# Taking over the last attention output and the first expert loads across a stage border, and moving one batch's sum and moments into layer 1

## The reference, cut to what matters

```python
x = L0_attn_X                                   # (4, 1024, 128)
xn = layernorm(x)
s = attention(xn, W_qkv, W_out)                 # 16 heads of 64
g = silu(moe(xn, router, 8 experts, top 2, shared expert))   # squared-ReLU MLPs, d_ff 512
x = x + s * g
xn = layernorm(x)
s = ssm(rmsnorm(xn) * norm_w, dt, A, Bmat, C, D)  # 64 states, causal decay filter
g = silu(ffn_fp4(xn, w_gate, w_up, w_down))     # FP4 block quantising, inner size 352
x = x + s * g
```

## Time and profile before

| | us |
|---|---|
| median of 3 runs | 1923.96 (1921.51 to 1924.07) |
| profiled execution, time | 1938.15 |
| its span | 1936.3 |
| PE busy | 1811.3 (94%) |
| DVE busy | 1512.7 (78%) |
| POOL busy | 1432.3 (74%) |
| ACT busy | 1002.9 (52%) |
| granted TensorE clock, mean | 0.98 |

### The profile page before, as it was taken

How to read it: one execution, slowest core, us unless ns; L and a number is a source line. 1 busy time by engine, 2 the same in 40 slices (tenths; PEclk the granted TensorE clock), 3 DMA queues, 4 the chain that set the end, 5 groups by cost and what they waited for, 6 DMA issues and landing times. The chain is left out here.

```text
span 1936.3 us, 33414 instructions
## 1 busy us (share of the span) xinstructions
PE 1811.3 (94%) x10522; PEld 1039.0 (54%) x10522; DVE 1512.7 (78%) x2052; ACT 1002.9 (52%) x1503; POOL 1432.3 (74%) x870
## 2 busy tenths in 40 slices
PE   5899999999999999999999999999999798985687
PEld 4455555555555555555555555555555476763456
DVE  6777777777777777777777777777777688879896
ACT  4345545445454454554544454545445488874553
POOL 4388888888888888888888888888888256655574
PEclk9899999999999999999999999999999899997899
DMA  7101010101001010101010110101010467531000
GB/s 245 45 12 55 12 57 16 54 22 43 31 35 54 11 54 11 54 12 58 15 54 22 43 35 32 54 11 54 11 54 12 164 217 223 171 93 57 1 17 28
DMA packets 98438, 108.95 MB, mean 56 GB/s; under 512 B 8161, under 2 KB 88097, under 8 KB 95202
## 3 DMA queue, kind: packets, MB, share of 16 engines
q1 hardware_dynamic: 93410, 98.26, 15.6%
q0 software_dynamic: 4992, 10.27, 1.5%
HBM read 53.12 MB, written 27.38 MB: 42 GB/s over the span
## 5 line engine op out<-in xcount | busy, mean ns | idle before, releaser
L1438 POOL TENSOR_TENSOR psum_k<-psum_k,probs 128x1024 f32<-128x1024 f32 x384 | 925.9, 2411 | 200.4 <-ACT probs L1383 185.3
L1455 DVE TENSOR_REDUCE mxh<-ps_m 128x2 f32<-128x1024 f32 x518 | 633.3, 1223 | 257.0 <-PE ps_m L1215 255.8
L1383 ACT ACTIVATE probs<-ps_s 128x1024 f32<-128x1024 f32 x512 | 497.2, 1023 | 265.7 <-PE ps_s L1232 212.9
L1240 PE MATMUL ps_v<-probs,V 128*64 128x512 f32 x2056 | 489.8, 597 | 0.0
L1479 DVE RECIPROCAL rden<-den 128x128 f32<-128x128 f32 x260 | 245.7, 946 | 25.2 <-ACT den L1352 16.0
L1240 PEld LDWEIGHTS ps_v<-probs,V 128*64 128x64 f32 x2056 | 137.5, 137 | 235.6 <-issue 229.7
L1215 PE MATMUL ps_m<-k_hi,q_hi 64*128 64x512 f32 x1036 | 237.6, 453 | 11.2 <-DVE mxh L1455 7.2
L1230 PE MATMUL ps_s<-q_lo,k_hi 64*128 64x512 f32 x1024 | 202.7, 390 | 0.0
L1230 PE MATMUL ps_s<-q_hi,k_hi 64*128 64x512 f32 x1024 | 202.3, 390 | 0.0
L1232 PE MATMUL ps_s<-shift,ones_r 64*128 64x512 f32 x1024 | 202.3, 388 | 0.0
L1230 PE MATMUL ps_s<-q_hi,k_lo 64*128 64x512 f32 x1024 | 202.0, 389 | 0.0
(11 more groups left out here) (309 smaller groups left out, 2803.4 us busy)
## 6 DMA issues: line engine op xcount, KB each, us to landing
e_ew<-w_split SPq DMA_DIRECT2D x23, 1024.0 KB
V<-V_next SPq DMA_DIRECT2D x33, 512.0 KB, 3.3
xs_hi<-xh SPq DMA_DIRECT2D x16, 512.0 KB, 3.7
xs_lo<-xl SPq DMA_DIRECT2D x16, 512.0 KB, 4.3
rows<-in_blank_d SPq DMA_DIRECT2D x4, 1483.5 KB, 16.2
e_x_raw<-rows SPq DMA_DIRECT2D x23, 258.0 KB
we_raw<-in_experts_d SPq DMA_DIRECT2D x33, 128.0 KB, 2.5
w_split<-we_hi SPq DMA_DIRECT2D x32, 128.0 KB, 1.9
```

Source lines behind the costliest of these rows:

```text
L1240: ins = nc.tensor.matmul(ps_v[rows, :], V[par][:, kt, rows], probs[:, t % RING, x, :], start=kt == 0, stop=kt == KT - 1)
L1383: nc.scalar.activation(probs[:, t % RING, :, :], ps_s[t % 2][:, :, :], ACT.Exp, scale=SCALE).then_inc(p_done, 1)
L1438: nc.gpsimd.tensor_tensor(acc, probs[:, (t - 1) % RING, :, :] if kt == 1 else acc, probs[:, t % RING, :, :], ALU.add).then_inc(add_done, 1)
L1455: nc.vector.tensor_reduce(mxh[:, kh, t, :], max_bank(unit, i)[:, :, :], AX.X, ALU.max).then_inc(m_done, 1)
```

## The change

The diff, cut to its core:

```diff
+def layer0_handed_on(nc, ctx, g):            # allocated ahead of attention, kept until layer 1
+    g.y_row = [sb(f"e_y_row{s}", [P, CH // P, D], F32) for s in range(4)]
+    g.den, g.rden, g.raw, g.attn = [y[:, :, :].rearrange("p t d -> p (t d)") for y in g.y_row]
+    x_raw = sb("e_x_raw", [P, 4 * (CH // P) * ROW], F32)
+    g.x_raw = [x_raw[:, s * (CH // P) * ROW:(s + 1) * (CH // P) * ROW] for s in range(4)]
+    g.V_next = x_raw[:, 0:TPB * 4 * DH].rearrange("p (t d) -> p t d", d=4 * DH)
+    g.w_first = [sb(f"e_ew{s}", [P, 4 * FF], F32R) for s in range(2)]
+    g.wo_last = sb("wo1", [P, D], F32)
 
 # expert_tiles, SP: the loads of tiles 0 and 1 leave
-            rows(0, 0)
-            weights(0, 0)
-            rows(0, 1)
-            weights(0, 1)
 # expert_tiles, PE
+            def last_output():
+                pe.wait_ge(last_attn, 1)
+                for x in range(2):
+                    rows = slice(x * DH, (x + 1) * DH)
+                    ins = nc.tensor.matmul(ps_y[rows, :], g.wo_last[:, rows], g.attn, start=True, stop=True)
+                ins.then_inc(last_out, 1)
 ...
+                        if isinstance(i, int) and at(i, s) == 0 and j == 2:
+                            last_output()
+                        if isinstance(i, int) and at(i, s) == 3 and j == 0:
+                            pe.wait_ge(last_added, 1)
 # expert_tiles, DVE
+                        if isinstance(i, int) and at(i, s) == 0 and j == 3:
+                            v.wait_ge(last_out, 1)
+                            nc.vector.tensor_tensor(g.sT[:, NT - CH:NT], ps_y[:, :], g.sT[:, NT - CH:NT], ALU.add).then_inc(last_added, 1)
 ...
+            last_inverse(0)
+            last_inverse(1)
             tokens(0, 0)
+            last_inverse(2)
+            last_inverse(3)
+            v.wait_ge(last_rden, 4)
+            nc.vector.tensor_tensor(g.attn, g.raw, g.rden, ALU.mult).then_inc(last_attn, 1)
             turns(v, body)
 ...
-            v.wait_ge(a_done, 4)
-            moments(nc, v, g, 1)
 # layer0_attention: even k_hi, k_lo, q_hi, q_lo lie in w_first
+    even = [w[:, k * T:(k + 1) * T] for w in g.w_first for k in range(2)]
-    LAST = ["out0", "den1", "out1"]
+    LAST = ["out0", "den1"]
 # layer0_attention, SP, behind its last waits
+            sp.wait_ge(scattered, 2 * TILES * 16)
+            sp.wait_ge(routed, 2)
+            load_rows(nc, sp, g, 0, 0)
+            sp.wait_ge(m_ready, KT + EARLY + N * STEPS)
+            sp.wait_ge(xv_done, reads(N - 1, "Q1"))
+            first = [sp.value_load(g.tile_w[0:1, s:s + 1], min_val=0, max_val=(E - 1) * P) for s in range(2)]
+            load_weights(nc, sp, g, first[0], g.w_first[0][:, :], 0)
+            load_rows(nc, sp, g, 1, 1)
+            load_weights(nc, sp, g, first[1], g.w_first[1][:, :], 1)
 # layer0_attention, DVE
             add_out(N, "out0")
-            for part in range(PARTS):
-                inverse(N, 1, part)
-            normalise(N, 1)
-            add_out(N, "out1")
 # layer1, POOL
-            inverse_std(nc, pool, g, 1)
             quantised_input(0, QS, 0)
+            pool.wait_ge(g.var_done, 2)
+            inverse_std(nc, pool, g, 1)
+            quantised_input(1, 2 * QS, 1, q_x12[0])
             inverse_rms(nc, pool, g, 1)
-            quantised_input(1, 2 * QS, 1, q_x12[0])
 # layer1, ACT
             rms_rows(0)
-            normalise(nc, act, g, 1)
             act.wait_ge(c_in, 4 * 16)
             normed_T(0)
             input_T(0)
             gates(0, 0)
             state_inputs(0)
-            rms_rows(1)
+            normalise(nc, act, g, 1)
             gates(0, 1)
             input_T(1)
             gates(1, 0)
+            rms_rows(1)
             normed_T(1)
             state_inputs(1)
 # layer1, DVE
             quantise(nc, v, q_step, 0, [(input_rows(0), *(a[:] for a in q_x))])
+            moments(nc, v, g, 1)
             quantise(nc, v, q_step, QS, [(input_rows(1), *q_x12[0])])
             moments(nc, v, g, 2)
```

More of the change, by code:

```diff
@@ L44, in attention_early @@
     g.wv_lo = sb("wv_lo", [P, PAIRS, 2 * DH], F32R)
-    g.wo = [sb(f"wo{i}", [P, D], F32) for i in range(2)]
+    g.wo = [sb("wo0", [P, D], F32), g.wo_last]
     g.probs = sb("probs", [P, RING, 2, CH], F32)
@@ L354, in _, with load_rows, load_weights @@
             layer1_weights()
+def layer0_handed_on(nc, ctx, g):
+    sb, pb, sem = g.scope(ctx)
+    g.y_row = [sb(f"e_y_row{s}", [P, CH // P, D], F32) for s in range(4)]
[5 more added lines that the diff above has]
+    g.wo_last = sb("wo1", [P, D], F32)
+    g.x_tile_in = [sem(f"e_x_in{s}") for s in range(4)]
+    g.w_tile_in = [sem(f"e_w_in{s}") for s in range(4)]
+def load_rows(nc, sp, g, tile, s):
+    dst = g.x_raw[s].rearrange("p (t d) -> p t d", d=ROW)
+    sp.dma_start(dst, g.rows[bass.ds(tile * CH, CH), :].rearrange("(n p) d -> p n d", p=P)).then_inc(g.x_tile_in[s], 16)
+def load_weights(nc, sp, g, first, w, s):
+    sp.dma_start(w.bitcast(F32), g.w_split[bass.ds(first, P), :]).then_inc(g.w_tile_in[s], 16)
 def layer1_early(nc, ctx, g):
@@ L361, in layer1_early @@
     g.wT_dn = sb("wT_dn", [P, 3, D], F32)
-    g.y_row = [sb(f"e_y_row{s}", [P, CH // P, D], F32) for s in range(4)]
     g.x_early = [sem(f"x_early{v}") for v in range(4)]
     g.w1_back = sem("w1_back")
-    g.x_raw = [sb(f"e_x_raw{s}", [P, CH // P * ROW], F32) for s in range(4)]
     g.xn_early = [g.x_raw[k][:, 0:CH // P * D].rearrange("p (t d) -> p t d", d=D) for k in range(2)]
@@ L496, in expert_tiles @@
     h_lo = sb("e_h_lo", [P, NH, CH], F32R)
-    w = [sb(f"e_ew{s}", [P, 4 * FF], F32R) for s in range(NS)]
+    w = g.w_first + [sb(f"e_ew{s}", [P, 4 * FF], F32R) for s in range(2, NS)]
     ws_raw = sb("e_ws_raw", [P, 2 * FF], F32)
     ws = sb("e_ws", [P, 4 * FF], F32R)
-    x_raw = [x[:, :].rearrange("p (t d) -> p t d", d=ROW) for x in g.x_raw]
+    x_raw = [x.rearrange("p (t d) -> p t d", d=ROW) for x in g.x_raw]
     x_hi = [sb(f"e_x_hi{s}", [P, CH], F32R) for s in range(NX)]
@@ L511, in expert_tiles @@
     ps_y = pb("e_ps_y", [P, CH])
-    w_in = [sem(f"e_w_in{s}") for s in range(NS)]
+    w_in, x_in = g.w_tile_in, g.x_tile_in
     ws_in = sem("e_ws_in")
@@ L516, in expert_tiles @@
     wslo_done = sem("e_wslo_done")
-    x_in = [sem(f"e_x_in{s}") for s in range(NS)]
+    last_rden = sem("e_last_rden")
+    last_attn = sem("e_last_attn")
+    last_out = sem("e_last_out")
+    last_added = sem("e_last_added")
     at_done = sem("e_at_done")
@@ L596, in rows @@
                     sp.wait_ge(at_done, at(i, s) - NS + 1)
-                sp.dma_start(x_raw[s][:, :, :], g.rows[bass.ds(at(i, s) * CH, CH), :].rearrange("(n p) d -> p n d", p=P)).then_inc(x_in[s], 16)
+                load_rows(nc, sp, g, at(i, s), s)
             def weights(i, s):
@@ L603, in weights @@
                     sp.wait_ge(down_done, NH + (at(i, s) - NS + 1) * FT)
-                sp.dma_start(w[s][:, :].bitcast(F32), g.w_split[bass.ds(first, P), :]).then_inc(w_in[s], 16)
+                load_weights(nc, sp, g, first, w[s][:, :], s)
             def sums(v):
@@ L960, in layer0_attention @@
     w_in, preset, w_staged, wlo_staged, add_done = g.attn_w_in, g.preset, g.w_staged, g.wlo_staged, g.add_done
-    k_hi, k_lo, q_hi, q_lo = ([sb(f"{name}{p}", [P, T], F32R) for p in range(2)] for name in ("k_hi", "k_lo", "q_hi", "q_lo"))
+    even = [w[:, k * T:(k + 1) * T] for w in g.w_first for k in range(2)]
+    k_hi, k_lo, q_hi, q_lo = ([even[k], sb(f"{name}1", [P, T], F32R)] for k, name in enumerate(("k_hi", "k_lo", "q_hi", "q_lo")))
     shift = [sb(f"shift{h}", [P, CH], F32R) for h in range(2)]
-    V_next = sb("V_next", [P, TPB, 4 * DH], F32)
+    V_next = g.V_next
     xs_hi = sb("xs_hi", [P, T], F32R)
     xs_lo = sb("xs_lo", [P, T], F32R)
[L966 to L969, removed]
+    den, rden, raw, attn = g.den, g.rden, g.raw, g.attn
     mxh = sb("mxh", [P, 2, 4, 2], F32)
@@ L2331, in program @@
             g.w1_out = sem("w1_out")
+            layer0_handed_on(nc, layer0, g)
             with ExitStack() as early:
```

5 lines of the change are left out of this document (4 added, 1 removed).

## The result

The change made the kernel slower. Its five runs gave a median of 1932.27 us (1931.71 to 1936.59), the kernel before 1923.96 on the same chip (1921.40 to 1931.21): a ratio of 1.0040 with a 95% interval of 1.0023 to 1.0056, so +7.7 us, between 4.4 and 10.8. The forecast was 1919.7 with a range of 1914.0 to 1925.5.

What follows compares the result with a forecast made beforehand. It took PE to bound the middle of the experts and chains of single instructions the borders. First border -10.0, experts' end -2.9 and layer 1 +8.6 gave -4.3 us: 1919.7 from 1923.96, range 1914 to 1925.5.

Steps and rivals of the forecast that it cites:

- PE going from tile to tile without a wait: Middle of the expert stage: PE is always busy, so a start earlier by x ends the stage x earlier.
- the 2.1 us of the border I leave as they are: Border from experts to layer 1: its 2.1 us stay unchanged when DVE ends earlier.
- Part 1: Border from attention to experts: early loads and the moved last output save time, -10.0 us taken.
- The block now ends with ACT's copy at 1518.15: End of attention: ACT's copy closes the block, the border takes 0.29 us, and experts begin at 1518.45.
- The -7.6 end: First border: smallest gain allowed, if entering the block costs 1.8 us for instruction fetch.
- The clock at this border: First border: PE's clock taken as lower, sum -9.4 us; at the full clock -12.4.
- Part 2: End of the experts: without `moments(1)` DVE ends at 1768.1 instead of 1770.99, -2.9 us.
- Part 3: Start of layer 1: `moments(1)` and the late `normalise(1)` delay every engine, +6.9 to +9.9, taken +8.6 us.
- up to 3.0. I take 1.7: Layer 1's start: PE's idle lowers the clock, lengthening the `gate_up` pairs and `state_T`; 1.7 us taken, up to 3.0.
- The *slower* one: Rival, expert tiles 2 and 3: late weights make PE wait, +8 us, total 1928; chance 0.13 with other causes.
- Layer 1 takes back what the border gives: Rival, both borders: entry costs 1.8, clock falls in both places, -7.6 + 7.0 = -0.6, 1923.4 us; chance 0.27.
- The first rival: First border's gain whole with clock kept up, layer 1 at its lower end: -8.4, 1915.6 us; chance 0.25.
- The last rival: Second border: `moments(1)` costs nothing in layer 1, -10.0 - 2.9 = -12.9, 1911 us; chance 0.05.

Runs made afterwards that it cites:

- e1: Changed kernel with `moments(1)` back in the experts and layer 1's lists as before, leaving the first border's part; 1928.88 us against 1932.40, ratio 0.9985.
- c0: The kernel before, unchanged, run again for a trace; 1934.35 us against 1932.40, ratio 1.0009.
- e4: e1 without POOL's drain at the ends of attention and experts; 1913.26 us against 1924.81, ratio 0.9947.
- e10: e1 with POOL's drain left out at attention's end alone; 1921.10 us against 1925.16, ratio 0.9977.
- e7: e1 with the last output back at attention's end, leaving the early loads and their buffers; 1925.78 us against 1924.81, ratio 0.9999.
- e3: Changed kernel without POOL's drain at the ends of attention and experts; 1929.99 us against 1932.40, ratio 0.9988.
- e2: Kernel before with only `moments(1)` and layer 1's lists changed, first border as before; 1944.07 us against 1932.40, ratio 1.0068.
- e9: Changed kernel with 32 added PE transposes ahead of `gate_up(1, 0)` in layer 1; 1932.43 us against 1925.16, ratio 1.0036.
- e6: Changed kernel with `rms_rows(1)` put directly behind `normalise(1)`; 1929.57 us against 1924.81, ratio 1.0026.
- e8: e7 with the loads back at the experts' start, leaving only the new buffer layout; 1929.41 us against 1925.16, ratio 1.0025.
- e11: The kernel of e4 run once more, on a second chip; 1924.90 us against 1935.42, ratio 0.9936.
- e5: Kernel before without POOL's drain at the ends of attention and experts; 1924.04 us against 1924.81, ratio 0.9997.

## Why the prediction was wrong

**What bounds the kernel now.** For the middle of the experts, "PE going from tile to tile without a wait" was a misreading: the 132.13 of 140.00 us hold waits of PE for ACT, up to 1.3 us each, in a profile that lay 14.2 us above the median. It is true of after's profile. The loop's length differs between profiles by more than the whole forecast, so whether an earlier start arrives whole at its end can't be read from one pair of them. At the borders I read the chain of DVE and took the hand-over to be 0.3 us at the first, and at the second "the 2.1 us of the border I leave as they are". The 2.1 were not a price of the border: they were the end of POOL's drain, which the timeline doesn't show, since it isn't counted as busy. The line of the block's end shows it in before's trace too (L590, above).

**Part 1, -10.0 predicted, -5.8 found** (distance A, 15.78 against 21.54; e1 against c0: -5.5), outside even the -7.6 to -12.4 that the sum allowed. Right: the loads at 1512.5, the chain behind the border (e4: 2.93 predicted 2.8), `last_output` counted whole. The step that failed is "The block now ends with ACT's copy at 1518.15". It ends with POOL's drain, and the first up came at 1528.21 - 2.57 = 1525.64 where the step had 1520.95. With the drain left out the sum comes out: A is 9.5 us shorter than before's in e4, where the clock fell, and 12.2 in e10, where it stayed up; the working had 9.4 and 12.4. Of the terms, with the drain in place, the loads gave 3.8 and the last output 1.6 to 2.0 (e7, e1, after). The -7.6 end was held open for a price of entering the block; PE's transposes start 1525.71 - 1525.34 = 0.37 us after the border, so there is none of that size. The stall at a taken branch of which the Trainium skill speaks ("Runtime: NRT & Kernel Launch", Instruction fetch mechanics) doesn't show at this border.

**The clock at this border.** I took the lower level, and after's trace has it: 0.50 in the first 4 us of matmuls. `last_output` took 1.08, not 1.98, since the clock was back by then.

**Part 2, -2.9 predicted, nothing found.** DVE's end did come earlier, 50.06 us behind its first weighting instead of 53.24, as the working said. The step that failed is "The 2.1 us of the border I leave as they are": POOL's last instruction didn't move (45.5 and 45.7 us behind the same point), its drain of 9.28 us didn't either, and the border grew to 5.09. e3 is the counter-test: without the drain the idle of 5.09 goes down to 0.51.

**Part 3, +8.6 predicted, +11.4 found** (39.01 against 27.59; alone in e2 39.51). The mechanism was right step by step, the sizes short. Measured from layer 1's first reduce, after against before:
- `gate_up(1, 0)` starts at 24.28 instead of 19.77, +4.5, where the working had 3.8. DVE's wait for `normalise(1)` was 3.13 instead of 2.3.
- `state_T(1)` starts at 31.23 instead of 22.25, +9.0, where the working had 6.9: on the 4.5 come `rms_rows(1)` with its hand-over, as predicted 3.0, and 1.5 for the pairs at the lower clock (e9, with the clock up, has the same stretch 1.5 shorter).
- `sizes` starts at +11.4: `state_T` itself 0.9 longer, and `state_up` 1.5 (3.44 instead of the 1.93 of e6). The term "up to 3.0. I take 1.7" of the clock left `state_up` out and was taken near its middle; it came to 1.5 + 0.9 + 1.5 = 3.9. That is the largest mis-sized term of this part, and e6 shows how it hangs on order: with `rms_rows(1)` ahead there is no idle before `state_T`, the clock is up there, and 5.5 us go in place of 3.0.

**Not in the prediction at all: where the buffers lie.** I had given the new layout no term. By time it costs +4.8 us (e8), which is as much as the early loads give.

**The sum.** By the traces: -5.8 + 0 + 11.4, and 1.9 of attention, gives +7.5; that it meets the measured value so closely is luck, since the 1.9 is a difference of means that overlap. By the times: +4.8 (e8), e7 against e8 (0.9999 - 1.0025) -5.0, e1 against e7 (0.9985 - 0.9999) -2.7, and e2's +13.1 make +10.2; each is uncertain by 2 to 3 us, and they come from several chips. Measured were +7.7 (4.4 to 10.8). The forecast of -4.3 was off by 12.0: 4.2 for Part 1, 2.9 for Part 2, 2.8 for Part 3, which leaves 2.1 for the layout (1.9 by attention's end, 4.8 by the time of e8).

**The rivals.** The *slower* one came true in its sign but not in its cause: PE has no idle at tiles 2 and 3, so the weights weren't late. "Layer 1 takes back what the border gives" was the nearest in mechanism; it had the border's gain too large (-7.6 for -5.8) and layer 1's loss too small (+7.0 for +11.4). The first rival had the clock kept at the border, which after's trace doesn't show, and +4.0 for the other two parts together, where +11.4 came. The last rival, `moments(1)` for nothing in layer 1, is excluded by e2.

**Left open.** Why POOL's drain lasts 5.3 us beyond POOL's last work in attention and 7.6 beyond it in the experts. Why the layout costs more than the DMA and attention times show. What puts the expert loop into the pattern in which PE waits; in the twelve profiles of the experiments it went with the chip, but before's and after's own differ in it on one chip. Why e4 and e11 gain more than their borders show, and e10 less.

## What to carry to other kernels

Before you move an instruction off the chain that ends a block, ask the trace for every engine's drain at the line where the block ends: the border comes when the last of them is through, and a gain ends where the next drain begins to count. Where POOL's is the last one, let POOL wait for its last writes by semaphore and leave the drain out, but together with the change that makes it late: alone that gave nothing that could be measured (e5). The earlier border gave 0.15% with both drains (e1, no change within its interval), 0.23% without the first (e10) and 0.53 to 0.64% without either (e4, e11). And work moved from a covered stretch into a list where engines take turns costs its own length plus every wait that it passes on; price it by walking through the lists of all engines. In the upper end of the range price every matmul group up to the next hand-over at the lower clock, not the first ones only: `state_T` and `state_up` were at it again behind their own idles, although the last pair before them had come back to the upper one (0.76).

## What the runs showed of the hardware

- POOL's drain at a block's end took 8.27 to 8.29 us in attention and 9.28 in the experts, of which 5.3 and 7.6 lay behind POOL's last work. In after's attention DVE's took 0.73, ACT's 0.63, SP's 0.13.
- The same instructions at the same border kept the upper clock in one execution and fell to the lower in another (e10 and e4); distance A, without the drain, was 9.31, 10.89, 10.89 and 12.00 us (e10, e3, e11, e4).
- With `state_T` at the upper clock in both (1.04 and 1.09) and 1.2 us of idle ahead in both, `state_up` took 1.93 us in e6 and 3.67 in e9. In e9 an idle of 2.88 stands in front of `state_T`; in e6 there is none, but one of 4.74 ahead of the pairs, where e9 has the 32 transposes.
- Moving buffers within the on-chip memory, with no other change, made 512 KB landings 9 to 11% slower (3.3 to 3.6, 3.7 to 4.1 us, the same in all profiles of either layout) and the kernel 0.25% slower.
- The end of layer 1, with the same instructions, kept the upper clock in some executions (1.00 in 20 us, c0 and e4) and not in others (0.74, e5, e7 and e11); from ACT's first `sizes` to the end it was 134.7 to 134.8 us in the first and 139.0 to 139.1 in the second.
